# A graph-and-scan kernel: twelve state buffers, a load ring of four, and quad sums, convolution halves, hand-over and residual moved by slots

## The reference, cut to what matters

```python
h = maximum(layernorm(x), 0)
x = x + relu(((adj * d[:, None] * d[None, :]) @ h) @ W.T + b)      # d = rowsum(adj)**-0.5
h = maximum(layernorm(x), 0)
g = layernorm(relu(adj @ h @ gcn_w + gcn_b)) * ln_g + ln_b
xz = g @ w_in                                    # 256 columns xc, 256 columns z
u = silu(causal_conv4(xc) + conv_b)
dt, B, C = softplus((u @ w_xp)[:, :8] @ w_dt + b_dt), ...          # B and C: 16 states each
s[t] = exp(dt[t] * A) * s[t-1] + dt[t] * B[t] * u[t]               # state: 256 channels x 16
y = ((s[t] @ C[t]) + u * D_skip) * silu(z)
out = x + y @ w_out
```

## Time and profile before

| what | value |
|---|---|
| median of three runs | 2566.11 us |
| the profiled execution | 2564.81 us |
| its span | 2563.0 us |
| granted TensorE clock, mean share of full speed | 0.956 |
| PE busy | 2206.2 us, 86% |
| DVE busy | 1995.6 us, 78% |
| ACT busy | 971.5 us, 38% |
| POOL busy | 1031.7 us, 40% |
| DMA | 683.36 MB, mean 267 GB/s |
| first and last L752 (slots 0 and 255) | 1458.2 and 2536.8 us |

### The profile page before, as it was taken

One profiled execution on the slowest core, in us unless ns is written; L12 is line 12 of the kernel. 1 busy time (PEld: TensorE's weight loads), 2 busy tenths in 40 slices (PEclk: granted clock), 3 DMA queues, 4 the chain that ended last, 5 costly groups with the idle time before them and its releaser, 6 DMA issues.

```text
span 2563.0 us, 21769 instructions
## 1 busy us (share of the span) xinstructions
PE 2206.2 (86%) x6736; PEld 1245.0 (49%) x6736; DVE 1995.6 (78%) x1999; ACT 971.5 (38%) x1696; POOL 1031.7 (40%) x550
## 2 busy tenths in 40 slices
PE   0337788999999999999999889899998899989866
PEld 0112334444447777878787334444444444444333
DVE  7899998897545666565655389989988899889886
ACT  0000000000014555455544455555555555555552
POOL 1101110111000000000000288888988899889665
PEclk9968899999999999999999999999999999999898
DMA  9999999999757555565554688988888888886221
GB/s 392 408 414 421 421 416 388 398 400 356 260 232 250 208 208 204 194 213 192 189 195 165 232 260 278 277 264 276 275 274 263 258 279 277 269 257 215 71 75 41
DMA packets 133090, 683.36 MB, mean 267 GB/s; under 512 B 14928, under 2 KB 15728, under 8 KB 80880
## 3 DMA queue, kind: packets, MB, share of 16 engines
q1 hardware_dynamic: 110592, 604.02, 63.0%
q0 software_dynamic: 5616, 40.90, 7.9%
q10 hardware_dynamic: 16768, 37.05, 3.9%
HBM read 624.76 MB, written 16.25 MB: 250 GB/s over the span
## 4 chain that ended last, share of the span: by engine, by line
PE 47%; POOL 23%; DMA 11%; issue 10%; DVE 7%; ACT 2%; POOLq 0%; ACTq 0%; SPq 0%; DVEq 0%
PE ps L914 19%; PE ps L833 14%; POOL arena L531 9%; DMA ring<-adj 6%; PE ps L954 6%; POOL ring L531 6%; DVE arena L655 4%; DMA arena<-adj 4%; PE ps L1032 3%; PE ps L984 2%; POOL arena L537 2%; POOL ring L537 1%; POOL arena L519 1%; POOL rstd L490 1%; POOL arena L546 1%
## 5 line engine op out<-in xcount | busy, mean ns | idle before, releaser
L914 PE MATMUL ps<-adj_parts,h_parts 128*128 128x512 f32 x2592 | 599.7, 393 | 11.7 <-ACT adj_parts L1129 11.4
L914 PEld LDWEIGHTS ps<-adj_parts,h_parts 128*128 128x128 f32 x2592 | 489.3, 189 | 119.5 <-ACT adj_parts L1129 13.9
L954 PE MATMUL ps<-ring,diag_h 128*128 128x512 f32 x1152 | 538.1, 599 | 0.0
L655 DVE TENSOR_TENSOR arena<-arena,ring 128x2048 f32<-128x2048 f32 x180 | 412.3, 2291 | 60.1 <-DMA ring<-adj 49.7
L833 PE MATMUL ps<-ring,arena 128*128 128x512 f32 x824 | 379.6, 619 | 56.0 <-DMA ring<-adj 56.0
L531 POOL TENSOR_TENSOR arena<-arena 128x1024 f32<-128x1024 f32 x156 | 373.6, 2401 | 90.9 <-ACT state L1193 90.4
L819 DVE TENSOR_TENSOR_SCAN arena<-arena,state,ps 128x512 f32<-128x512 f32 x312 | 381.8, 1265 | 26.9 <-PE ps L984 16.9
L674 DVE TENSOR_TENSOR adj_parts<-ring,adj_parts 128x1024 fp32r<-128x1024 f32 x216 | 264.2, 1225 | 97.9 <-ACT adj_parts L1129 87.0
L1201 ACT ACTIVATE arena<-arena,a_sb 128x512 f32<-128x512 f32 x512 | 338.5, 709 | 0.5
L752 DVE TENSOR_TENSOR ps<-arena,ps 128x1024 f32<-128x1024 f32 x256 | 309.8, 1210 | 37.0 <-PE ps L975 37.0
L954 PEld LDWEIGHTS ps<-ring,diag_h 128*128 128x128 f32 x1152 | 219.9, 194 | 240.2 <-issue 236.0
(11 more groups left out here) (108 smaller groups left out, 2215.4 us busy)
## 6 DMA issues: line engine op xcount, KB each, us to landing
ring<-adj SPq DMA_DIRECT2D x452, 1024.0 KB, 9.2
arena<-c_scratch SPq DMA_DIRECT2D x128, 512.0 KB, 5.1
diag_h<-adj SPq DMA_DIRECT2D x32, 1024.0 KB, 12.6
arena<-adj SPq DMA_DIRECT2D x28, 1024.0 KB, 16.6
arena<-arena POOLq DMA_DIRECT2D x16, 1024.0 KB, 11.8
arena<-x ACTq DMA_DIRECT2D x16, 512.0 KB, 7.6
arena<-ring POOLq DMA_DIRECT2D x8, 1024.0 KB, 12.3
ring<-ring POOLq DMA_DIRECT2D x8, 1024.0 KB, 11.5
```

The costliest lines, as they stand in the source:

```text
L655: nc.vector.tensor_tensor(acc, acc, v, ALU.add).then_inc(adds_done, 1)
L914: last = nc.tensor.matmul(acc[:, c, :], h_parts[:, blk % 2, layer, h_part, a * F:(a + 1) * F], adj_parts[:, buf, adj_part, c * MM:(c + 1) ...
L954: last = nc.tensor.matmul(acc_c[k % 2] if k >= 2 else y_ps[:, k, :], tile_of(h1, PJ * p + j), blk[:, j * T:(j + 1) * T], start=first and j ...
```

## The change

- HSB 10 to 12 and RING_C 5 to 4: six buffer pairs, three in the arena as before and three in the ring; four ring slots for loads in phase C. The fourth load ahead is left out: 20 instead of 24 units before the first slot.
- QSUM (9, 9, 9, 7) to (11, 11, 10, 8).
- Slots of the side work: GCN, BIAS two earlier, STATS, AGGREGATE, NORMALISE, TRANSPOSE one earlier; XZ from four slots in a row to -13, -11, -9, -8; SKIP, GATE, STORE one later, RESIDUAL one later; the products end three slots sooner, and the hand-over comes three slots after a chunk's last unit instead of two.
- SPLIT stands behind the scans in DVE's slot; w of chunk 0 is made by DVE, not POOL; chunk 0's SiLU of u comes right after its second convolution half.
- In phase B `layer1_input` comes behind piece 9 instead of 7, but for the first strip.

```diff
--- before.py
+++ after.py
@@ -42,7 +42,7 @@
 
 RING = 7
 RING_A = RING + 1
-RING_C = 5
+RING_C = 4
 
 T = 512
 NCH = N // T
@@ -60,18 +60,18 @@
 LN_EPS = 1e-5
 DEG_EPS = 1e-9
 
-HSB = 10
+HSB = 12
 
 AHEAD = 12
 
 KEPT = 1
 DEGREE = 1
 
-GCN, BIAS, STATS, AGGREGATE, NORMALISE = -24, -23, -22, -18, -17
-TRANSPOSE, XZ, SILU, DBC, SPLIT = -13, -12, -8, -7, -6
+GCN, BIAS, STATS, AGGREGATE, NORMALISE = -26, -25, -23, -19, -18
+TRANSPOSE, XZ, SILU, DBC, SPLIT = -14, (-13, -11, -9, -8), -8, -7, -6
 DT, SOFTPLUS, WEIGHTED_U = -5, -4, -3
-QSUM, NSUM = (9, 9, 9, 7), 6
-LOAD_X1, SKIP, GATE, OUT, RESIDUAL, STORE = 22, 20, 21, 30, 31, 32
+QSUM, NSUM = (11, 11, 10, 8), 6
+LOAD_X1, SKIP, GATE, OUT, RESIDUAL, STORE = 22, 21, 22, 30, 32, 33
 
 PJ = 2 * JT
 S1B = 3
@@ -113,9 +113,9 @@
     pairs_of = {k: list(range((k // CPS + 1) * BPS // 2)) for k in range(NCH)}
     for k in (2, 3):
         pairs_of[k] = pairs_of[k][BPS // 2:] + pairs_of[k][:BPS // 2]
-    loads += [("C", k, p) for k in (2, 3) for p in pairs_of[k][:BPS // 2]]
+    loads += [("C", k, p) for k, n in ((2, BPS // 2), (3, 1)) for p in pairs_of[k][:n]]
     loads += [("C", k, p) for k in (0, 1) for p in pairs_of[k]]
-    loads += [("C", k, p) for k in (2, 3) for p in pairs_of[k][BPS // 2:]]
+    loads += [("C", k, p) for k, n in ((2, BPS // 2), (3, 1)) for p in pairs_of[k][n:]]
     loads += [("C", k, p) for k in range(4, NCH) for p in pairs_of[k]]
     load_at = {key: q for q, key in enumerate(loads)}
 
@@ -159,33 +159,33 @@
     products = {g: [] for g in slots}
     units = {k: [(k, p, j) for p in pairs_of[k] for j in range(PJ)] for k in range(NCH)}
     ahead = BPS // 2 * PJ
-    products[FIRST_SLOT - 1] = units[2][:ahead] + units[3][:ahead] + units[0]
-    rest = units[1] + units[2][ahead:] + units[3][ahead:] + [unit for k in range(4, NCH) for unit in units[k]]
+    products[FIRST_SLOT - 1] = units[2][:ahead] + units[3][:PJ] + units[0]
+    rest = units[1] + units[2][ahead:] + units[3][PJ:] + [unit for k in range(4, NCH) for unit in units[k]]
 
 
     handover = {0: FIRST_SLOT}
-    end = DS * (NCH - 1) + GCN - 1
+    end = DS * (NCH - 1) + GCN - 2
     n, due = 0, 0.0
     for g in range(FIRST_SLOT, end):
         due += (len(rest) - n - due) / (end - g) if g > DBC else n < len(units[1])
         while due >= 1 - 1e-6 and n < len(rest):
             k, p, j = rest[n]
             last = (p, j) == (pairs_of[k][-1], PJ - 1)
-            if k > 3 and g < handover.get(k - 2, end) or last and g + 2 < DS * (k - S1B) + GCN + 6:
+            if k > 3 and g < handover.get(k - 2, end) or last and g + 3 < DS * (k - S1B) + GCN + 6:
                 break
             products[g].append(rest[n])
             n, due = n + 1, due - 1
             if last:
-                handover[k] = g + 2
-                assert g + 2 <= DS * k + GCN
+                handover[k] = g + 3
+                assert g + 3 <= DS * k + GCN
     assert n == len(rest)
     block_end = {load_at["C", k, p]: g for g in slots for k, p, _ in products[g]}
 
 
     misc = []
     for g in range(FIRST_SLOT, LAST_SLOT):
-        for stage, kinds in ((GCN, ["gcn"]), (OUT, ["out"]), (TRANSPOSE, ["tr"]), (XZ, ["xz0"]), (XZ + 1, ["xz1"]),
-                             (XZ + 2, ["xz2"]), (XZ + 3, ["xz3"]), (DBC, ["dbc"]), (DT, ["dt0"]),
+        for stage, kinds in ((GCN, ["gcn"]), (OUT, ["out"]), (TRANSPOSE, ["tr"]), (XZ[0], ["xz0"]), (XZ[1], ["xz1"]),
+                             (XZ[2], ["xz2"]), (XZ[3], ["xz3"]), (DBC, ["dbc"]), (DT, ["dt0"]),
                              (DT + 1, ["dt1"])):
             k = chunk_at(g, stage)
             if k is not None:
@@ -510,7 +510,7 @@
                 if k is not None:
                     norm_scale(3 * NS + k, CT)
                 k = chunk_at(g, WEIGHTED_U)
-                if k is not None:
+                if k:
                     if k >= 2:
 
                         pool.wait_ge(dbu_done, DS * (k - 1))
@@ -776,15 +776,6 @@
                 if k is not None:
                     dve.wait_ge(stats_done, k + 1)
                     aggregate(CT)
-                k = chunk_at(g, SPLIT)
-                if k is not None:
-
-                    dve.wait_ge(bc_high, k + 1)
-                    low = parts[k % 2][LOW:KD, :]
-                    nc.vector.tensor_tensor(low, misc_of("dbc", k)[LOW:KD, :], low.bitcast(F32), ALU.subtract)\
-                        .then_inc(misc_free, 1)
-
-
                 for h in range(HALVES):
                     k = chunk_at(g, SKIP + h)
                     if k is None:
@@ -818,6 +809,17 @@
                     for h in range(HALVES):
                         nc.vector.tensor_tensor_scan(hs[g % HSB][:, h, :], da[g % 3][:, h, :], dbu_ps[g % 2][:, h, :],
                                                      state[:, h, n:n + 1], ALU.mult, ALU.add).then_inc(scan_done, 1)
+
+                k = chunk_at(g, SPLIT)
+                if k is not None:
+
+                    dve.wait_ge(bc_high, k + 1)
+                    low = parts[k % 2][LOW:KD, :]
+                    nc.vector.tensor_tensor(low, misc_of("dbc", k)[LOW:KD, :], low.bitcast(F32), ALU.subtract)\
+                        .then_inc(misc_free, 1)
+                if chunk_at(g, WEIGHTED_U) == 0:
+                    dve.wait_ge(dt_ready, 1)
+                    nc.vector.tensor_tensor(w[0], dt[0], u[0], ALU.mult).then_inc(w_ready, 1)
 
 
         @block.tensor
@@ -1021,7 +1023,7 @@
                         last = nc.tensor.transpose(m_ps[:, t * P:(t + 1) * P], gbuf[:, t, :], ident[:, :])
                     last.then_inc(misc_full, 1)
                 for c in range(2 * HALVES):
-                    k = chunk_at(g, XZ + c)
+                    k = chunk_at(g, XZ[c])
                     if k is not None:
                         evacuated(pe, "tr", k)
                         m_ps = use_misc((f"xz{c}", k))
@@ -1170,7 +1172,7 @@
 
                     if m == (1 if n == 1 else 0):
                         move_layer1(n - 1, i + 1)
-                    if m == 7:
+                    if m == (7 if n == 1 else 9):
                         layer1_input(n)
             move_layer1(NS - 2, 0)
             layer1_input(NS - 1)
@@ -1184,6 +1186,10 @@
                 src = misc_of(*key)[0:dst.shape[0], :]
                 nc.scalar.activation(dst, src, ACT.Identity if more else ACT.Copy, **more)\
                     .then_inc(misc_free, 1)
+
+            def silu_u(k):
+                evacuated(act, "xz1", k)
+                nc.scalar.activation(u[k % 2], cv, ACT.Silu).then_inc(u_ready, 1)
 
             for g in range(FIRST_SLOT, LAST_SLOT):
                 if 1 <= g <= NCH * DS:
@@ -1232,20 +1238,22 @@
                             .then_inc(halo_done, 1)
                     evacuate(("tr", k), h_t[:, CONV:CONV + T], scale=ln_sb[:, 0:1], bias=ln_sb[:, 1:2])
                 for c in range(2 * HALVES):
-                    k = chunk_at(g, XZ + c)
+                    k = chunk_at(g, XZ[c])
                     if k is None:
                         continue
                     if c < HALVES:
 
                         evacuate((f"xz{c}", k), cv[:, c, :], bias=cols_sb[:, 0, c:c + 1], scale=1.0)
+                        if (c, k) == (1, 0):
+                            silu_u(0)
                     else:
                         if k >= 2:
                             act.wait_ge(yg_ready, k - 1)
                         evacuate((f"xz{c}", k), sz[k % 2][:, c - HALVES, :])
                 k = chunk_at(g, SILU)
                 if k is not None:
-                    evacuated(act, "xz1", k)
-                    nc.scalar.activation(u[k % 2], cv, ACT.Silu).then_inc(u_ready, 1)
+                    if k:
+                        silu_u(k)
                     evacuated(act, "xz3", k)
                     nc.scalar.activation(sz[k % 2], sz[k % 2], ACT.Silu).then_inc(sz_ready, 1)
                 k = chunk_at(g, DBC)
```

## The result

In runs taken side by side the kernel before took 2570.56 us (median of 14, 2562.94 to 2573.43), the changed one 2576.09 us (median of 14, 2567.13 to 2583.98): a ratio of **1.0029, 95% interval 1.0016 to 1.0042**. The forecast was 2530. The profiled execution has a span of 2569.2 us, against 2563.0 before.

What follows compares the result with a forecast made beforehand. POOL with its own accumulating DMA was taken as the bound. Terms -7.1, -1.1, -0.6, -12, -6 and -9.7 sum to -36.5 on 2564.8, giving 2528.3; with the runs' median 1.3 above, 2530 us, range 2500 to 2553.

Steps and rivals of the forecast that it cites:

- Accumulating DMA: Quad chunks: landing taken at its present means, bounds 9.3 and 14.0 us, since bytes per chunk stay the same.
- Rival D: Quad chunks: DMA lands at 14.0 us, issued beside C rows and held-back ring loads; loop 71.9, 2590 us; chance 0.09.
- mild case: Quad chunks, between the forecast and the full Rival D: landing of 12.5 us, 2548 us.
- The loop that bounds: Quad chunks: POOL with its own accumulating DMA bounds, 68.3 us a chunk, becoming 67.3; -12 us.
- Lead of layer 1: Phase B: layer 1's input normalised two pieces later shortens five of six ACT stops, 5 x 1.42 = -7.1 us.
- Lead of the scan: Before the first scan slot: 20 products ahead instead of 24, first hand-over and B row 0 sooner; -1.1 us.
- Change-over: Last quad add to slot 216: from 33.1 us to 25, or 28.4 if PE starts at 1.2 GHz; -6 us.
- Last forty slots: End of the scan: skip's (7.6 us) and residual's (2.1) waits go, both coming a slot later; -9.7 us.
- Ring of four: Scan stage: ring loads issued at least 15.4 us before use, against landings of 5.3 to 14.0; cost 0.
- PE's slots 2 to 5: Quad chunks: 20.3 us of PE work against DVE's 15.2, 1.9 uncovered; DVE stays under POOL's 67.3; cost 0.
- rival E: Quad chunks: the ring of four starves PE in most chunks, 1 us each; 2542 us; chance 0.05.
- C: Quad chunks: no gain, PE's slots 2 to 5 or 1.2 GHz clock eat 1 us; 68.0 stays, 2542; chance 0.22.

Runs made afterwards that it cites:

- the late add: On the changed kernel, first and second quad add behind rows 7 and 11 instead of 6 and 10: 2501.7 us, ratio 0.9743; on the kernel before: 2557.6, 0.9951.

## Why the prediction was wrong, point by point

**The step that failed:** "*Accumulating DMA.* Its landing under the new order has no row. Bounds: 9.3 and 14.0; taken at its present means, since bytes per chunk stay the same". Bytes per chunk did stay the same. But the landing also hangs on what is issued beside the DMA, and the change moved SP's ring loads there. Windows forecast at 11.6 + 12.0 = 23.6 measured 14.1 + 12.6 = 26.7: 3.1 us in 13 chunks are 40 us. The gap from 2530 to 2576 is 46, and 4.5 of it is that the kernel before took 2570.6 in these runs instead of 2566.1. The experiment that takes the load out of the window after row 3 gives the cross-check: 2535.6.

**Rival D was this mechanism**, with its place ("C rows and held-back ring loads", released by the same multiplications) and its point: it "decides from a mean landing of about 13.2 us on". The mean over both windows was 13.3, the loop 70.3 against D's 71.9, and the time between its mild case (2548) and its full one (2590). Of the two transfers that it named, the ring loads matter and the C rows hardly. Its chance, 0.09, was too small. The landings after row 11, 12.5 on the mean where POOL is furthest behind, were the evidence in hand; the first table above could have been made from the 39 DMAs of the kernel before alone, whose 16 with a load within that time of them land after 13.0 us on the mean and the other 23 after 11.2. I had read their mean and not what went out beside them.

**The loop that bounds** was named rightly for the changed kernel, and in part for the kernel before, where the late add uncovered DVE's own 67.9 us a chunk right behind POOL's 68.3. POOL's four pieces stayed within 0.05 us, its waits for states turned into waits for landings, DVE's waits at quad sums fell from 27.9 to none, and none of DVE's gain reached the end. The prediction overlooked that w, made in POOL's row 13, caps DVE's lead (55.3 us of waits). That was harmless: it came from POOL's lag, and with the late add it is 1.6 us.

**Lead of layer 1:** forecast -7.1, measured -11.1 alone. The gaps came out as forecast: PE's waits for ACT in phase B are 3.7 us where rows 5 have 11.4. Of the 3.7, 1.9 is the first strip's, unchanged, and the other five gaps are 0.37 us each, near the 0.45 that I let stand (so they are not gone whole, as I wrote ahead of that run). That gives 7.6 us. The rest is TensorE's clock, which the forecast left out. Behind four of the six gaps of 1.9 us the clock granted to PE was at 1.2 GHz for 3.4 us; behind the short gaps it stayed at 2.4. First the stretch behind the gap that ends at 1264.4 in the kernel before, then the stretch around its counterpart, which ends at 1260.2 in the changed one (columns as in rows 1; third from the end is the clock's share of full speed):

```profile
1266.20:1269.60 3.40, 3.40 (x9) 2.69 (x9) 0.57 (x1) 0.51 (x2) 0.00 (x0) 0.50 0.48 157
1257.00:1270.00 13.00, 12.56 (x54) 9.78 (x53) 6.40 (x9) 7.77 (x16) 0.00 (x0) 1.00 0.55 175
```

The changed kernel has one such stretch left in phase B, behind the first strip's gap. Three fewer, at half of 3.4 us each, are an estimated 5.1 us. With the 7.6 that makes 12.7. Measured from its first to its last matmul of phase B, PE took 12.3 us less; it began 1.1 us later, so phase B ended 11.2 us sooner.

**Lead of the scan:** forecast -1.1, and -12.9 - (-11.1) = -1.8 came. **Change-over:** -4.2 of -6; from the last quad add to slot 216 took 28.9 us. That it is near the 28.4 that had PE start at 1.2 GHz is luck: the granted clock was back at 2.4 GHz 1.3 us after the add began and stayed there. The terms listed for this path add up to 17.7 us and not to 25, and PE had indeed ended the second conv half 19.2 us after the add began. But slot 216 doesn't hang on that: DVE has six slots to run through there, and stands still for only 3.6 us of the 28.9. Before, it stood for 6.2, of which 3.1 for the last products, and was 2.3 us further behind when the add began. **Last forty slots:** -5.0 of -9.7. DVE's waits from slot 216 to 255:

```profile
DVE arena L787 <- PE ps L997: 2.2, 1, 2.2
DVE parts L818 <- ACT parts L1266: 2.1, 2, 1.1
DVE ps L752 <- POOL arena L519: 1.0, 1, 1.0
```

The residual's wait is gone and the skip's went from 7.6 to 2.2, so 7.5 of the 9.7 came. But split and w wait there now (3.1 us), which before they didn't. That leaves 4.4, and DVE's work in the stretch is 0.6 us less: the 5.0. **Ring of four and PE's slots 2 to 5:** forecast 0. PE's waits for ring loads in the whole scan stage:

```profile
PE ps L956 <- DMA ring<-adj: 2.5, 2, 1.4
```

So rival E didn't come, and C (DVE waiting above 50 us for B rows while POOL waits for states) neither: 30.9 and 6.9.

## What to carry to other kernels

A loop bound by a DMA's landing has to be costed with what is issued beside that DMA. Sort its landings by the distance to the nearest other transfer before taking a mean, and see who shares its release. A queue with an in-order wait in front bunches transfers just behind the event that ends the wait. And use the time of the wait before shortening the transfer: one row's work moved in front of the consumer was worth 74 us, all that was done to the landing itself 29 to 40. (In the kernel before, where another bound stood 0.4 us behind, the same row was worth 0.5%.) With a bound gone, price the next edit on the engine that then bounds: the same move of w gained 16 us under POOL's bound and lost 20 under DVE's.

## What the runs showed of the hardware

- A 1 MB accumulating DMA from SBUF to SBUF, issued by POOL, lands in 10.5 to 10.7 us on the mean when the nearest 1 MB ring load is more than 3 us away, and in 13.0 when one is issued from 2 us before to 0.6 us after it; single ones go from 8.1 to 15.7. With the nearest load 1.5 to 3 us later it is 10.9, with the nearest 2 to 3.2 us earlier 12.0. With ring loads held back until it had landed it took 10.9 instead of 14.1.
- In phase B of the kernel before, waits of 1.9 us on PE were followed in four of six cases by 3.4 us at a granted clock of 1.2 GHz; in the changed kernel the five waits of 0.37 us were followed by none.
- The same multiplication w (two inputs in SBUF) takes DVE 1.23 us for chunk 0, when POOL is idle, and 1.97 at the median, up to 2.40, in the kernel with w on DVE and the late add, mostly beside POOL's multiplications (in the one with w on DVE alone 2.11, up to 3.80):

```profile
L817 DVE TENSOR_TENSOR arena<-arena x16: 1224/1972/2397, 1444.7 to 2429.4; 128x1024 f32<-128x1024 f32 x16
```

The Trainium skill, page "SBUF — State Buffer", section "Who interferes with whom", says that a DVE instruction with two SBUF inputs contends with a GpSimd instruction that reads SBUF; the trace agrees (1.97 against 1.23), and DVE's other multiplications, with one input in PSUM, stay at 1.21.
